# A post-norm transformer layer on one core: attention normalised along features, with the head sums and quotients carried through HBM

## The reference, cut to what matters

```python
# x: 32 x 512 x 256; 16 heads of 16 features; hidden size 768
def attention(x, Wqkv, Wout):
    q, k, v = split(x @ Wqkv)
    logits = einsum('bihd,bjhd->bhij', q, k) / 4 + slope[h] * (j - i)
    attn = softmax(where(i >= j, logits, -inf), axis=-1)
    return einsum('bhij,bjhd->bihd', attn, v).reshape(B, T, D) @ Wout

def ffn(x, w_gate, w_up, w_down):        # int32 weights, scaled by 1/127
    return (silu(x @ wg.T) * (x @ wu.T)) @ wd.T

x = layernorm(x + attention(x))
x = layernorm(x + ffn(x))
```

## Time and profile before

| | |
|---|---|
| profiled execution, whole | 2136.29 us |
| its span (first to last instruction) | 2134.6 us |
| median of three executions | 2135.81 us |
| TensorE, matmuls | 1983.0 us, 93% |
| VectorE | 1595.1 us, 75% |
| ScalarE | 1223.5 us, 57% |
| GpSimd | 928.5 us, 43% |
| DMA engines, mean share of queue 1 | 48.5% |

### The profile page before, as it was taken

One profiled execution on the slowest core, in us unless ns is written; L12 is line 12 of the kernel. 1 busy time (PEld: TensorE's weight loads), 2 busy tenths in 40 slices (PEclk: granted clock), 3 DMA queues, 4 the chain that ended last, 5 costly groups with the idle time before them and its releaser, 6 DMA issues.

```text
span 2134.6 us, 47883 instructions
## 1 busy us (share of the span) xinstructions
PE 1983.0 (93%) x19236; PEld 1550.0 (73%) x19236; DVE 1595.1 (75%) x2765; ACT 1223.5 (57%) x1999; POOL 928.5 (43%) x1924
## 2 busy tenths in 40 slices
PE   4779999999999999999999999999999999999986
PEld 3557777777777777777777777777877877777766
DVE  4557777787777787777778777778777778777754
ACT  1446656555655656655655665565565665566552
POOL 0123444444444453444454444444344445444444
PEclk8789999999999999999999999999999999999998
DMA  7455455355555445545545545545554544553500
GB/s 205 103 120 105 101 112 118 96 112 114 115 112 110 103 108 106 128 103 108 113 100 112 121 109 111 116 97 114 106 122 109 106 109 102 111 125 91 100 16 21
DMA packets 148830, 229.09 MB, mean 107 GB/s; under 512 B 13552, under 2 KB 64496, under 8 KB 148592
## 3 DMA queue, kind: packets, MB, share of 16 engines
q1 hardware_dynamic: 148608, 226.02, 48.5%
HBM read 139.98 MB, written 84.93 MB: 105 GB/s over the span
## 4 chain that ended last, share of the span: by engine, by line
PE 80%; DVE 10%; ACT 5%; DMA 2%; issue 1%; SPq 1%; POOL 0%; POOLq 0%; DVEq 0%
PE pair L495 72%; PE pair L498 8%; DVE row_max L801 7%; ACT probs L726 3%; DVE staged_lo L786 2%; ACT staged_hi L704 2%; DMA q_rows<-max_lo 1%; SPq L471 0%; DMA q_rows<-bounce 0%; DMA probs<-L_attn_Wout 0%; SPq L480 0%; DMA bounce<-staged_lo 0%; DVE row_max L803 0%; DVE xt_lo L786 0%; DVE x1t_lo L786 0%
## 5 line engine op out<-in xcount | busy, mean ns | idle before, releaser
L726 ACT ACTIVATE probs<-pair 128x1024 f32<-128x1024 f32 x640 | 627.1, 1027 | 150.1 <-PE pair L495 149.8
L903 POOL TENSOR_SCALAR_AFFINE_SELECT probs<-probs 128x256 f32<-128x256 f32 (+1 forms) x896 | 371.5, 440 | 445.9 <-ACT probs L726 445.1
L910 POOL TENSOR_TENSOR h_lo<-h_full,h_hi 128x256 fp32r<-128x256 f32 x384 | 283.2, 738 | 507.6 <-ACT h_hi L751 496.9
L803 DVE TENSOR_REDUCE row_max<-pair 128x8 f32<-128x1024 f32 x256 | 312.6, 1221 | 115.2 <-PE pair L495 114.7
L801 DVE TENSOR_REDUCE row_max<-pair 128x2 f32<-128x1024 f32 x256 | 311.9, 1218 | 71.2 <-PE pair L495 71.2
L495 PE MATMUL pair<-q_rows,k_rows 64*128 64x512 f32 (+3 forms) x2048 | 321.0, 370 | 38.4 <-DMA q_rows<-max_lo 20.8
L495 PE MATMUL pair<-k_rows,q_rows 52*128 52x512 f32 (+3 forms) x2048 | 299.6, 351 | 60.2 <-DVE staged_lo L786 26.1
L495 PE MATMUL pair<-probs,v_ones 128*32 128x512 f32 (+3 forms) x4096 | 319.3, 441 | 0.8 <-ACT probs L726 0.8
L495 PEld LDWEIGHTS pair<-q_rows,k_rows 64*128 64x128 f32 x2048 | 167.8, 188 | 157.2 <-ACT probs L726 92.2
L495 PEld LDWEIGHTS pair<-k_rows,q_rows 52*128 52x128 f32 x2048 | 179.0, 190 | 122.9 <-DVE row_max L801 62.9
L704 ACT ACTIVATE staged_hi<-pair 128x512 fp32r<-128x512 f32 x128 | 76.6, 599 | 269.9 <-PE pair L495 260.5
(11 more groups left out here) (88 smaller groups left out, 3622.7 us busy)
## 6 DMA issues: line engine op xcount, KB each, us to landing
bounce<-staged_hi SPq DMA_DIRECT2D x128, 256.0 KB
bounce<-staged_lo SPq DMA_DIRECT2D x128, 256.0 KB
q_rows<-bounce SPq DMA_DIRECT2D x128, 256.0 KB, 5.2
k_rows<-bounce SPq DMA_DIRECT2D x128, 256.0 KB, 6.2
x_sb<-L_attn_x SPq DMA_DIRECT2D x32, 512.0 KB, 10.4
k_rows<-bounce SPq DMA_DIRECT2D x128, 128.0 KB, 5.5
q_rows<-bounce SPq DMA_DIRECT2D x128, 128.0 KB, 6.7
x<-L_attn_x SPq DMA_DIRECT2D x32, 512.0 KB, 9.1
```

The source lines that it names most:

```text
L726: scalar.activation(probs[g][:, tile, :, :], pair[:, :, :], ACT.Exp, scale=scale).then_inc(s_exp, 1)
L803: vector.tensor_reduce(maxima[:, QB2_PARTS:QB0 + 1, :, p].rearrange("p b s -> p s b"), pair[:, :, :].rearrange("p s (b n) -> p s b n", n=P ...
L903: made = pool.affine_select(out=diagonal, in_=diagonal, compare_op=ALU.is_ge, fill=0.0, base=0, pattern=[[0, diagonal.shape[1]], [1, P]], ...
L910: pool.tensor_tensor(h_lo[:, m, :], h_full[(n_split_h[step] - 1) % H_BUFFERS][:, :], h_hi[:, m, :].bitcast(F32), ALU.subtract).then_inc(s_ ...
```

## The change

The result of `pv` is no longer transposed on TensorE. `pv_t[g]` is sent to an HBM buffer (`send`, SP, after each `pv_copy`), and `fetch` (SP, once both groups of a unit are there) reads it back with the 128 features of the unit on partitions (`attn`), and the eight rows of sums as 128 x 32 (`sums`). VectorE takes the reciprocal of these (`recip`), `send_recip` stores it, `fetch_recip` reads it back with each head's row repeated for its 16 features (`recips`). GpSimd multiplies (`divide`, 128x512), ScalarE rounds (`attn_hi`, 128x512) and GpSimd subtracts (`attn_lo`, 128x512). The TensorE transposes `attn`, their splits and the two `divide` steps of VectorE are gone. For unit `u` the sends are in windows `u+1` and `u+2`, `recip` in window `u+2`, `fetch_recip` at its end, `divide` in window `u+3`.

The feed-forward of a batch runs one window later (halves in windows 2b+5 and 2b+6), so there is one more window in all; `rest` now has one written order for both kinds of window. The window that carries the out-projection has `gate_up` first, and the other has x1's transposes first. `values` stand ahead of `down`. The statistics of the first norm are a step of their own (`stats1`), behind the last `gate_up` and the projection. `norm1` stays behind `down`. The result's DMA (`store_out`) goes, like the second `norm1`, behind the fifth `scores` tile of the next attention part (`norms_due`); before, it stood at `norm2`'s own place, ahead of `spread`. `store_max` is two DMAs instead of four, issued by ScalarE two steps behind `max_row`.

```diff
         self.user, self.used = [None] * BANKS, list(range(-BANKS, 0))
-        for w in range(-2, self.units + 4):
+        for w in range(-2, self.units + 5):
             self.attention(w)
             self.rest(w)
+        self.norms()
...
                     self.resume(("pv", u, g, 1), ("pv", u, g, 0))
                     self.add("pv_copy", u, g)
+                    self.add("send", u, g)
+                    if g == 1:
+                        self.add("fetch", u)
...
     def max_row(self, u):
         if self.has(u):
             self.split("max_row", u)
-            self.add("store_max", u)
...
     def rest(self, w):
-        k = w // 2
-        ffn, part = k - 2, w % 2
+        k, part = w // 2, 1 - w % 2
+        ffn = k - 2 - part
         has_ffn = 0 <= ffn < self.batches
+        has_out = part == 1 and 0 <= k - 2 < self.batches
         if self.has(w + 1):
             self.add("gather", w + 1)
+        if self.has(w - 3):
+            self.add("divide", w - 3)
         if part == 0:
-            if 0 <= k < self.batches:
-                self.values(k)
             if has_ffn:
                 self.transposed("x1", ffn)
-            self.turn(w - 2, 1)
-            self.turn(w - 1, 0)
-            if 0 <= k - 1 < self.batches:
-                self.add("load_residual", k - 1)
-            if 0 <= k + 1 < self.batches:
-                self.transposed("x", k + 1)
-                if k + 2 < self.batches:
-                    self.add("load_x", k + 2)
-            if has_ffn:
-                self.gate_up(ffn, 0, range(0, 2))
-            self.max_row(w)
-            if has_ffn:
-                self.gate_up(ffn, 0, range(2, 6))
             self.project(w + 2, 0)
-            if has_ffn:
-                self.down(ffn, 0)
-            self.project(w + 2, 1)
-        else:
-            done = k - 1
-            has_done = 0 <= done < self.batches
-            self.turn(w - 2, 1)
-            self.project(w + 2, 0)
-            self.turn(w - 1, 0)
             if w == -1:
                 self.ffn_weights()
-            if has_done:
-                self.transposed("attn", done)
-            if has_ffn:
-                self.gate_up(ffn, 1, range(0, 3))
             self.max_row(w)
-            if has_done:
-                self.project_out(done, 0)
-            if has_ffn:
-                self.gate_up(ffn, 1, range(3, 6))
-            if has_done:
-                self.project_out(done, 2)
-            if has_ffn:
-                self.down(ffn, 1)
-            if has_done:
-                self.add("norm1", done, 0)
-                self.norms_due.append(("norm1", done, 2))
-            self.project(w + 2, 1)
+        if has_ffn:
+            self.gate_up(ffn, part, range(0, 2))
+        if self.has(w - 3):
+            self.add("attn_hi", w - 3)
+            self.add("attn_lo", w - 3)
+        if part == 1:
+            self.max_row(w)
+        if self.has(w - 2):
+            self.add("recip", w - 2)
+            self.add("send_recip", w - 2)
+        if part == 0 and 0 <= k - 1 < self.batches:
+            self.add("load_residual", k - 1)
+        if has_ffn:
+            self.gate_up(ffn, part, range(2, 3))
+        if self.has(w):
+            self.add("store_max", w)
+        if part == 1 and 0 <= k + 1 < self.batches:
+            self.transposed("x", k + 1)
+            if k + 2 < self.batches:
+                self.add("load_x", k + 2)
+        if has_ffn:
+            self.gate_up(ffn, part, range(3, 4))
+        if has_out:
+            self.project_out(k - 2, 0)
+            self.project_out(k - 2, 2)
+        if has_ffn:
+            self.gate_up(ffn, part, range(4, 6))
+        if part == 1:
+            self.project(w + 2, 0)
+        elif 0 <= k + 1 < self.batches:
+            self.values(k + 1, 0)
+            self.values(k + 1, 2)
+        if has_out:
+            self.add("stats1", k - 2, 0)
+            self.add("stats1", k - 2, 2)
+        if has_ffn:
+            self.down(ffn, part)
+            self.norms_due.append(("store_out", ffn, part))
+        if has_out:
+            self.add("norm1", k - 2, 0)
+            self.norms_due.append(("norm1", k - 2, 2))
+        self.project(w + 2, 1)
+        if self.has(w - 2):
+            self.add("fetch_recip", w - 2)
 
     def ffn_weights(self):
         self.add("as_float")
...
         row_max = [sb(f"row_max{i}", [P, MAX_PLANES, 2, UNIT_PAIRS]) for i in range(2)]
         max_hi, max_lo = sb("max_hi", [UNIT_HEADS, tokens], F32R), sb("max_lo", [UNIT_HEADS, tokens], F32R)
         pv_t = [sb(f"pv_t{i}", [P, tokens]) for i in range(2)]
-        rden = [sb(f"rden{i}", [P, blocks, GROUP]) for i in range(2)]
-        attn = [sb(f"attn{i}", [P, blocks, dim]) for i in range(2)]
+        attn = [sb(f"attn{i}", [P, tokens]) for i in range(2)]
+        recips = [sb(f"recips{i}", [P, tokens]) for i in range(2)]
+        sums = [sb(f"sums{i}", [P, UNIT_HEADS * tokens // P]) for i in range(2)]
...
         bounce = nc.dram_tensor("bounce", [2, 4, HEAD_DIM, UNIT_PAIRS, 2, tokens], F32, kind="Internal").ap()
+        pv_bounce = nc.dram_tensor("pv_bounce", [2, 2, GROUP, 2, HEAD_DIM, tokens], F32, kind="Internal").ap()
...
         CONSTS_READY, SPLIT_W_READY, SPLIT_W_DONE, AS_FLOAT = 6, 2, 4, 3
 
...
                             r = s * HALF + r0 * HEAD_DIM
                             sync.dma_start(rows[r:r + n * HEAD_DIM, :, :].bitcast(F32),
                                            bounce[z, n0:n0 + n, :, :, s, :].rearrange("n d p t -> (n d) p t")).then_inc(s_gathered[z], 16)
-                elif kind == "store_max":
-                    u, = key
-                    e.wait_ge(s_hi, n_hi["split_hi", "max_row", u])
-                    e.wait_ge(s_lo, n_lo["split_lo", "max_row", u])
-                    for r, source in enumerate((max_hi, max_lo)):
-                        for s in range(2):
-                            row = s * HALF + MAX_ROW + r
-                            sync.dma_start(q_rows[u % 2][row:row + 1, :, :].bitcast(F32),
-                                           source[s * UNIT_PAIRS:(s + 1) * UNIT_PAIRS, :].bitcast(F32)).then_inc(s_max_stored[u % 2], 16)
-                elif kind == "norm2":
+                elif kind == "send":
+                    u, g = key
+                    z = u % 2
+                    e.wait_ge(s_pv_copy, n_pv_copy["pv_copy", u, g])
+                    if u >= 2:
+                        e.wait_ge(s_fetched[z], (u // 2) * 16 * 2)
+                    sync.dma_start(pv_bounce[z, g].rearrange("h c d t -> (h c d) t"), pv_t[g][:, :]).then_inc(s_sent[z][g], 16)
+                elif kind == "fetch":
+                    u, = key
+                    z = u % 2
+                    for g in range(2):
+                        e.wait_ge(s_sent[z][g], (u // 2 + 1) * 16)
+                    if u >= 2:
+                        e.wait_ge(s_attn_lo, n_attn_lo["attn_lo", u - 2])
+                        e.wait_ge(s_recip, n_recip["recip", u - 2])
+                    parts = pv_bounce[z].rearrange("g h c d t -> (g h) c d t")
+                    sync.dma_start(sums[z][:, :], parts[:, 1, 0, :].rearrange("h (a n) -> h a n", n=sums[z].shape[1])).then_inc(s_fetched[z], 16)
+                    sync.dma_start(attn[z][:, :], parts[:, 0, :, :]).then_inc(s_fetched[z], 16)
+                elif kind == "send_recip":
+                    u, = key
+                    z = u % 2
+                    e.wait_ge(s_recip, n_recip["recip", u])
+                    if u >= 2:
+                        e.wait_ge(s_recip_fetched[z], (u // 2) * 16)
+                    sync.dma_start(recip_bounce[z].rearrange("h (a n) -> h a n", n=sums[z].shape[1]), small_recips[z][:, :]).then_inc(s_recip_sent[z], 16)
+                elif kind == "fetch_recip":
+                    u, = key
+                    z = u % 2
+                    e.wait_ge(s_recip_sent[z], (u // 2 + 1) * 16)
+                    if u >= 2:
+                        e.wait_ge(s_divide, n_divide["divide", u - 2])
+                    r = recip_bounce[z]
+                    wide = bass.AP(tensor=r.tensor, offset=r.offset, ap=[list(r.ap[0]), [0, HEAD_DIM], list(r.ap[1])])
+                    sync.dma_start(recips[z][:, :], wide).then_inc(s_recip_fetched[z], 16)
+                elif kind == "store_out":
                     b, part = key
-                    e.wait_ge(s_norm2, 2 * n_norm2[step])
+                    e.wait_ge(s_norm2, 2 * n_norm2["norm2", b, part])
                     sync.dma_start(out[b, part * 2 * P:(part + 1) * 2 * P, :].rearrange("(t p) d -> p t d", p=P),
                                    result[part][:, :, :]).then_inc(s_result_out[part], 16)
...
-                elif kind == "turn":
-                    u, g = key
-                    bank = bank_of(step)
-                    e.wait_ge(s_pv_copy, n_pv_copy["pv_copy", u, g])
-                    for t in range(blocks):
```

(64 more changed lines are left out.)

45 lines of the change are left out of this document (20 added, 25 removed).

## The result

The changed kernel takes 2224.53 us (median of four, 2220.43 to 2232.18) against 2135.43 us of the kernel before: 1.0422 times as long, 95% interval 1.0406 to 1.0437. I had forecast 2074 us, range 2044 to 2125. The profiled execution has a span of 2226.1 us.

What follows compares the result with a forecast made beforehand. TensorE, busy 96% of the steady stretch, was taken as the bound: 2134.6 - 83.8 (transposes) + 19 (new stalls) + 3 (start and end) = 2072.8 us of span, forecast 2074 us, range 2044 to 2125.

Steps and rivals of the forecast that it cites:

- What bounds the kernel: Whole kernel: TensorE bounds it, busy 96% of the steady stretch; the chain repeats every 63.23 us, one batch of two windows.
- what goes: TensorE: 768 transposes of pv_t and attn removed at 0.109 us each, 83.8 us; VectorE's saved work counted as nothing.
- What comes on the path: TensorE in rest: new stalls of 0.4 us (x1's split) and 0.2 us (out-projection), 19 us over some 31 batches.
- What is covered: stats1, values, norm1, the new transfers (some 7 us of wire time per window) and store_max's issues: counted as nothing.
- the sign of being wrong: Period per batch: forecast 61.2 us; the prediction is wrong if it is over 62 or under 60.6 us.
- Late gather: SP's queue: send behind spread delays fetch, then the gather, so TensorE waits; slower, 2170 or 2240 us; chance 0.16.
- a margin of 2.4 us: Gather on SP's queue: with send landing in 2.7 us, the gather lands at 1069.2, 2.4 us early.
- the case: fetch and fetch_recip, 8 outermost, use half the engines: 256 KB takes 3.6 us, not 1.8; gather 2.6 us late, 2240 us.
- ScalarE on the path: ScalarE: store_max's issues, with attn_hi's wait ahead, delay tanh in even windows; 38 us more, 2112 us; chance 0.11.
- Nothing: TensorE: removed transposes had covered splits that now stall it as long; 2135 us, needs 2.6 us a batch; chance 0.07.
- Start and end: First windows and tail: one more window, partly offset by savings early on; net +3 us, bounds -8 and +12.
- my +9: Tail: the feed-forward half moved out of the first full window, about six tiles and down, adds about 9 us.

Runs made afterwards that it cites:

- e_c16: Changed kernel with fetch and fetch_recip at 16 instead of 8 outermost, partitions ordered (feature, head), Wout's rows permuted to match: 2097.32 us, ratio 0.9806 to the kernel before.
- e_lateattn: Changed kernel with the 256 KB of features fetched at the end of rest, the sums left in place: 2099.12 us, ratio 0.9834 to the kernel before.
- e_spmax: Changed kernel with store_max issued by SP instead of ScalarE, same place, still two DMAs: 2238.56 us, ratio 1.0472 to the kernel before.
- b_max: Kernel before with store_max alone changed, to two DMAs issued by ScalarE right behind max_row: 2168.55 us, ratio 1.0148 to the kernel before.
- p_values: Changed kernel with 16-outermost reads, values put back at the head of rest instead of ahead of down: 2111.21 us, ratio 0.9883 to the kernel before.

## Why the prediction was wrong, step by step

**What bounds the kernel, and what goes.** Right. With the transfers mended the period is 61.22 us, 1.95 us less than before. TensorE's waits for x1's split, the gather and the maxima, 17.8 us in 29 batches, are 0.6 us of a batch; 2.62 - 0.6 = 2.0. So the transposes came off at about their full 2.62 us, and the rate out of the chain, 0.109 us, was the right one.

**What comes on the path.** Right in kind, a little high. x1's split: 9.3 us in 29 waits in e_c16, 0.3 us each, where I took 0.4. The GpSimd steps of 128x512 took 1.284 and 1.288 us, and TensorE waited 8.6 us for `attn_lo` in all, none of it between 200 and 1970 us; I took 0.2 us a batch.

**What is covered: the step that failed.** I set 1.06 MB at 146 GB/s to 7 us of wire time in a window of 31 and called it covered because "most of a window lies between each of these transfers and its user". Two things were wrong with that. In the steady stretch the transfers do not hinder their own users but those of the transfers behind them: the gather, and `store_max` (90.2 us of waiting, where I had put nothing). And a read is not priced by its bytes alone: e_c16, with the same bytes in the same order of SP and 16 instead of 8 outermost, is 127 us faster than the changed kernel. The period, 65.49 us, is beyond the 62 that I had set as the sign of being wrong.

**The rivals.** "Late gather" had the mechanism and the place: the queue behind `spread`, the send landing late, 256 KB ahead of the gather. Its 16% were far too few. I had found a margin of 2.4 us by pricing the send at 2.7 us, the landing of a store that was issued into an idle queue, though the same paragraph said that this one is not. In the profile `fetch` waited 5.3 us. Counted from the last split of the window before (1040.80 before, 1039.51 in the changed kernel's chain), the gather's first issue came 15.4 us later instead of 14.5: SP was 1 us late, no more. But the gather's last landing grew from 7.0 to 10.8 us. I had weighed the landing as a constant, with 1.8 us for the bytes ahead of it, and only the issue as movable. It was also not the gather that ended last but the store of the maxima behind it, in every second window; of the 4.3 us of a batch, 3.3 are waiting (90.2 us in 27 waits of the steady stretch). The remaining 1 was not measured apart; the lower clock is enough for it, since 4 us at 0.58 are some 1.7 us of work lost (an estimate from the window above). The time, 2224.5 us, lies between the two that I had worked out for this rival, 2170 and 2240.

The two sentences on the Trainium skill (DMA: Bandwidth & Descriptors, section "Why a DMA increments its semaphore by 16 and not by 1") were the ones to believe. By that rule the count of 8 confines a transfer to half of the engines. The traces agree: a DMA share of 0.53 against 0.97, and 8 packets more for each read that goes from 8 to 16. So do the times, of 2224 to 2097, 2224 to 2116, 2224 to 2173 and 2328 to 2206 us; only behind e_lateattn, where the features' read was already out of the way, is the step small, 2099 to 2094. It also fits ScalarE's queue on the page of the profile: 1280 packets for 128 DMAs are 10 each, of which 8 are the eight rows of data, leaving two, one for each of two engines if its outermost count of 2 decides.

I had put the case in a sentence beside the sum and given it no weight of its own, because "No row of before has such a shape of this size". That was wrong. `spread` writes 256 KB four times in each window, and its side in HBM, `bounce[z, n].rearrange("d p s t -> (p s) d t")`, has 4 x 2 = 8 outermost. A window laid over it in the kernel before, when nothing else is in flight:

```profile
1046.60:1052.00 5.40, 5.04 (x70) 2.72 (x74) 4.61 (x5) 3.56 (x4) 5.04 (x14) 1.00 0.52 180
```

Half of the engines, visible before the change was made. It also shows that the share is not the price: these 8 engines move 180 GB/s, more than the 146 of the gather's stretch, so my 3.6 us for 256 KB on half of them was no better than the 1.8. `spread`, the send's neighbour in the queue, keeps its 8 in every kernel here; no run tries it with 16.

"ScalarE on the path" did not set the changed kernel's time: with SP issuing instead (e_spmax) it was no faster. b_max shows the case where the step stands closer behind `max_row`, p_values where `down` has no cover. "Nothing", the removed transposes as cover, did not happen either.

**Statistics and values.** I counted `stats1` at nothing, as work that is merely moved. In e_c16 its place is worth 39 us and that of `values` 14 us. Both parts of the change are good; I had seen that they cover something and had not asked what the kernel would be without them.

**The clock.** I had no term for it. TensorE's clock is 0.96 to 0.97 over the steady stretch of the changed kernel and 1.00 in e_c16; the fall to 0.58 at 1074 follows the idle 3.5 us at 1069.5.

**Start and end.** +3 us was the net of terms of which the one for the end was mis-sized most. Windows from `combine` of unit 63 to the end, kernel before, e_c16, changed kernel:

```profile
2035.10:2134.60 99.50, 73.31 (x585) 63.40 (x584) 48.58 (x126) 39.24 (x83) 47.80 (x91) 0.89 0.06 20
```

```profile
1975.20:2096.00 120.80, 82.57 (x629) 72.07 (x628) 51.58 (x134) 44.16 (x97) 64.10 (x110) 0.88 0.13 41
```

```profile
2100.60:2226.00 125.40, 87.21 (x628) 74.89 (x628) 51.61 (x133) 44.02 (x97) 64.08 (x110) 0.82 0.13 39
```

From before to e_c16 the end grows by 21.3 us: 9.3 us of TensorE's busy time (my +9, the feed-forward half that moves there) and 12.0 us of idle time around it, which I had named ("waits are bare") and not priced. The start gave 3.3 us back (203.1 to 199.8), where I had 5.5. In the changed kernel the end is longer still, at a clock of 0.82. Which wait of the end holds the 12 us was not tried apart.

With the measured +18 in place of my +3 the sum is 2089 us, and e_c16 took 2097; the rest is mostly that I had counted the gain for all 32 batches, where the table has 29 in the steady stretch.

## What to carry to other kernels

Work that is traded for DMA is not priced by bytes over a mean rate: look at what is queued behind the new transfer on its queue, how near to its user that lands today (here the gather's last piece, issued at 1059.8 and landing after 7.0 us, some 5 us before its user at 1072.9), and treat that landing as a number that grows. Count the outermost dimension of both sides of every new access pattern; where it is small, reorder the partitions and let a weight's rows absorb the permutation, which costs one more DMA at the start. Moving the read out of the way did as much (e_lateattn), and needs no new layout. And when a long wait is removed by experiment, expect the next one close behind it: only what comes ahead of all of them, here the fetch, gave nearly the whole gain.

## What the hardware showed that I had not expected

A read of 256 KB with 8 outermost, right ahead of the gather, cost 108 us over 64 windows more than the same read with 16. That is 3.4 us for each of the 32 windows in which TensorE waited, about twice the 1.8 us of its bytes at 146 GB/s; the other read cost 52 us, 1.6 in each of them. Transfers with 8 outermost kept the DMA share at 0.52 to 0.53, the read with 16 at 0.97.

A small store on another engine's queue did not overtake: `store_max` was issued on ScalarE's queue at 1060.70 and 1061.24 us, had 16 KB each to move, and the second landed 11.8 us later, at 1073.00, after the gather that SP had issued from 1054.95 to 1060.0. From 1060.7 to 1069.9 us not one packet of ScalarE's queue was moved, and all 20 of the two stores ran from there to 1073. So the stores waited to be started; they were not slow in moving. What they waited for, and whether the residual's 512 KB, issued at 1061.45 on SP's queue, held them up, these runs don't tell.

The idle 3.5 us were followed, from 1074 to 1078 us, by a mean granted clock of 0.58, so a late transfer costs TensorE more than the wait itself.
